# A transformer block on one core: score rows of a pair's two heads on separate halves of the partitions

## The reference

```python
ada = silu(c) @ W_ada + b_ada                      # 6 vectors of 288 for each sequence
shift_msa, scale_msa, gate_msa, shift_mlp, scale_mlp, gate_mlp = split(ada, 6)
h = layernorm(x) * (1 + scale_msa) + shift_msa
q, k, v = split(h @ W_qkv + b_qkv)                 # 16 heads, D = 18
attn = softmax((q * D**-0.5) @ k.T)                # 256 x 256 for each head
x = x + gate_msa * ((attn @ v) @ W_proj + b_proj)
h = layernorm(x) * (1 + scale_mlp) + shift_mlp
x = x + gate_mlp * (gelu(h @ W_fc1 + b_fc1) @ W_fc2 + b_fc2)   # FF = 1152
```

## Time and profile before

| | |
|---|---|
| median of 3 runs | 1230.65 us (1229.91 to 1230.84) |
| time of the profiled execution | 1228.32 us |
| its span | 1226.5 us |
| TensorE busy | 96% of the span; weight loads 87% |
| VectorE, ScalarE, GpSimd busy | 74%, 71%, 44% |

### The profile page before, as it was taken

How to read it: one execution, slowest core, us unless ns; L and a number is a source line. 1 busy time by engine, 2 the same in 40 slices (tenths; PEclk the granted TensorE clock), 3 DMA queues, 4 the chain that set the end, 5 groups by cost and what they waited for, 6 DMA issues and landing times.

```text
span 1226.5 us, 27564 instructions
## 1 busy us (share of the span) xinstructions
PE 1181.1 (96%) x9863; PEld 1064.3 (87%) x9863; DVE 901.8 (74%) x1928; ACT 866.1 (71%) x1485; POOL 540.3 (44%) x557
## 2 busy tenths in 40 slices
PE   6888999999999999999999999999999999999977
PEld 5666999999998999999999999999999999997777
DVE  5687777877777787778777777777777787775553
ACT  5387777777777777777777777777777777778721
POOL 3012544444454444445454444444444445443364
PEclk9799999999999999999999999999999999999999
DMA  8554555554555554445555444555554555444220
GB/s 265 171 169 138 167 167 164 164 154 144 163 160 159 168 166 145 157 157 162 167 166 164 147 159 150 166 165 167 161 153 148 158 166 159 162 149 140 87 68 20
DMA packets 134330, 188.91 MB, mean 154 GB/s; under 512 B 24544, under 2 KB 102422, under 8 KB 133947
## 3 DMA queue, kind: packets, MB, share of 16 engines
q1 hardware_dynamic: 134033, 186.71, 48.3%
q10 hardware_dynamic: 162, 0.44, 0.1%
HBM read 121.92 MB, written 64.63 MB: 152 GB/s over the span
## 4 chain that ended last, share of the span: by engine, by line
PE 84%; SPq 5%; DMA 4%; DVE 3%; ACT 2%; issue 1%; POOL 0%; ACTq 0%; POOLq 0%; DVEq 0%
PE a_bank L867 10%; PE x_bank L785 10%; PE score_bank L808 9%; PE turn_bank L834 9%; PE st_bank L822 9%; PE b_bank L867 8%; PE b_bank L881 6%; PE b_bank L882 5%; PE b_bank L883 5%; PE a_bank L848 4%; PE x_bank L793 4%; SPq L623 2%; DMA qk_rows<-qst 1%; DMA ql<-zeros 1%; PE x_bank L759 1%
## 5 line engine op out<-in xcount | busy, mean ns | idle before, releaser
L1138 DVE TENSOR_REDUCE mx<-score_bank 128x2 f32<-128x512 f32 x512 | 342.0, 687 | 95.8 <-PE score_bank L808 93.7
L953 ACT ACTIVATE e<-st_bank 128x1024 f32<-128x1024 f32 x256 | 262.4, 1025 | 125.8 <-PE st_bank L822 123.5
L1287 POOL TENSOR_TENSOR gl<-gl_raw,gh 128x512 fp32r<-128x512 f32 (+1 forms) x160 | 194.3, 1221 | 226.4 <-DVE gh L1203 226.4
L946 ACT CAST ql<-mxt 4x256 fp32r<-4x256 f32 x512 | 206.2, 403 | 7.4 <-DVE mxt L1147 0.6
L808 PEld LDWEIGHTS score_bank<-kl,ql 122*128 122x128 f32 x1024 | 146.9, 190 | 42.0 <-issue 24.4
L808 PE MATMUL score_bank<-kl,ql 122*128 122x256 f32 x1024 | 174.6, 293 | 5.6 <-DMA ql<-zeros 3.3
L881 PE MATMUL b_bank<-w,gh 128*128 128x288 f32 x576 | 174.5, 303 | 2.2 <-DVE tmp L1209 1.9
L822 PE MATMUL st_bank<-ql,kl 122*128 122x512 f32 x512 | 165.7, 405 | 7.7 <-ACT e L953 6.9
L882 PE MATMUL b_bank<-w,gh 128*128 128x288 f32 x576 | 170.5, 296 | 0.0
L883 PE MATMUL b_bank<-w,gl 128*128 128x288 f32 x576 | 170.3, 296 | 0.0
L834 PE MATMUL turn_bank<-e,ve 128*32 128x256 f32 x2048 | 123.8, 382 | 0.3 <-ACT e L953 0.3
(11 more groups left out here) (152 smaller groups left out, 2473.1 us busy)
## 6 DMA issues: line engine op xcount, KB each, us to landing
qk_rows<-qst SPq DMA_DIRECT2D x128, 256.0 KB, 5.3
ql<-qk_rows SPq DMA_DIRECT2D x384, 72.0 KB
kl<-qk_rows SPq DMA_DIRECT2D x378, 72.0 KB
o_rows<-on SPq DMA_DIRECT2D x128, 128.0 KB
gate<-gates SPq DMA_DIRECT2D x32, 432.0 KB, 4.4
xin<-in_x SPq DMA_DIRECT2D x32, 288.0 KB, 5.9
x<-in_x SPq DMA_DIRECT2D x32, 288.0 KB, 3.0
out<-x SPq DMA_DIRECT2D x32, 288.0 KB, 4.5
```

The costliest lines, as they stand in the source:

```text
L946: last = nc.scalar.copy(rows[:, :, :, t, a, :], src)
L953: nc.scalar.activation(e[:, j % 4, :, :, :].rearrange("p u i l -> p (u i l)"), st_bank[:, :, :, :].rearrange("p u i l -> p (u i l)"), ACT. ...
L1138: nc.vector.tensor_reduce(mx[:, j // HP, i, :, col:col + 1], score_bank[i][:, :].rearrange("p (t l) -> p t l", t=NT), AX.X, ALU.max).then_ ...
L1287: nc.gpsimd.tensor_tensor(gl[:, cols], g[:, cols], gh[:, cols].bitcast(F32), ALU.subtract).then_inc(g_lo, 1)
```

## The change

What it does:

- A tile of 64 partitions for each head of a pair (TILE = 64): rows 0 to 3 of a tile are the max rows, rows 4 to 57 the q or k rows, KM = 58. Head 0 has partitions 0 to 57, head 1 partitions 64 to 121. ql no longer holds the heads apart and no longer has zeros for the other head, so its slot is half as large.
- s: four matmuls as before, of 58 rows each, in the order head 0, head 1, head 0, head 1. st: four matmuls of 256 columns instead of two of 512, heads in turn as well. The two heads of a pair write different banks of PSUM.
- Four slots instead of three. The thirteenth read (zeros) is gone, READS = 12, with its memory buffer. In its place GpSimd clears 68 partitions x 1024 of the slot, in a new step **clr** (twice in a period, after ln2_stats), which waits until the st steps of the half that used the slot are done. qkr waits for clr.
- kl's max rows are set once, at the start, by four ScalarE copies over 68 partitions in place of four small DMAs.
- mb: eight copies of 4 partitions as before, sorted by head instead of by row tile.
- The order of the steps on all engines is unchanged but for clr and for what qkr no longer has.

```diff
-MXR = 64
-HB = MXR + PAIRS // 2
-KM = HB + KS
+TILE = 64
+KM = PAIRS // 2 + KS
-SLOTS = 3
+SLOTS = 4
-READS = 13
+READS = 12
...
 POOL_ORDER = [
...
-    ("proj", -1, 0), ("proj", -1, 1), ("sum2", -2, 0), ("ln2_stats", -1, 0), ("bias", -1, 0), ("lt", -1, 0),
-    ("sum2", -2, 1), ("xt", 3, 0), ("fc1", -1, 0),
+    ("proj", -1, 0), ("proj", -1, 1), ("sum2", -2, 0), ("ln2_stats", -1, 0), ("clr", 2, 0), ("clr", 2, 1),
+    ("bias", -1, 0), ("lt", -1, 0), ("sum2", -2, 1), ("xt", 3, 0), ("fc1", -1, 0),
...
-        ql = sb("ql", [P, SLOTS, 2, HP, L], F32R)
+        ql = sb("ql", [P, SLOTS, HP, L], F32R)
-        e = sb("e", [P, 4, NT, 2, L])
+        e = sb("e", [P, 4, 2, NT, L])
...
-                    if use == 0:
-                        sp.wait_ge(consts, ROWS_SET)
-                        wait(sp, rows_cleared, slot)
-                    else:
-                        before = b * HALVES + half - SLOTS
-                        sp.wait_ge(st_full, PAIRS * (before // HALVES) + HP * (before % HALVES + 1))
-                if m == 12:
...
-                        sp.dma_start(ql[MXR:MXR + HP, slot, :, :, :].rearrange("p i j l -> p (i j l)").bitcast(F32),
-                                     zero_dram).then_inc(qk_rows[slot], 16)
-                    return
+                    if b == 0 and half == 0:
+                        sp.wait_ge(kl_chosen, SLOTS)
+                    sp.wait_ge(ql_cleared, HALVES * b + half + 1)
...
                 for i in range(2):
                     wait(pe, s_max[i], PAIRS * b + j)
-                    for t in range(NT):
+                for t in range(NT):
+                    for i in range(2):
+                        rows = slice(TILE * i, TILE * i + KM)
                         last = nc.tensor.matmul(score_bank[i][:, t * L:(t + 1) * L],
-                                                ql[0:KM, slot, i, j % HP, t * P:(t + 1) * P], kl[0:KM, slot, j % HP, :],
+                                                ql[rows, slot, j % HP, t * P:(t + 1) * P], kl[rows, slot, j % HP, :],
                                                 start=True, stop=True)
-                    last.then_inc(s_full[i], 1)
+                        if t == NT - 1:
+                            last.then_inc(s_full[i], 1)
...
                 for u in range(NT):
-                    last = nc.tensor.matmul(st_bank[:, u, :, :], kl[0:KM, slot, j % HP, u * P:(u + 1) * P],
-                                            ql[0:KM, slot, :, j % HP, :], start=True, stop=True)
+                    for i in range(2):
+                        rows = slice(TILE * i, TILE * i + KM)
+                        last = nc.tensor.matmul(st_bank[:, i, u, :], kl[rows, slot, j % HP, u * P:(u + 1) * P],
+                                                ql[rows, slot, j % HP, :], start=True, stop=True)
                 last.then_inc(st_full, 1)
...
+            def clear(b, half):
+                slot, use = half_use(b, half)
+                if use:
+                    before = b * HALVES + half - SLOTS
+                    pool.wait_ge(st_full, PAIRS * (before // HALVES) + HP * (before % HALVES + 1))
+                    nc.gpsimd.memset(ql[0:TILE + HP, slot, :, :].bitcast(F32), 0.0).then_inc(ql_cleared, 1)
```

More of the change, by code:

```diff
@@ L158 @@
     ("ln1_stats", 0, 0), ("xt", 0, 0), ("ln1_stats", 1, 0), ("xt", 1, 0), ("ln1_stats", 2, 0), ("xt", 2, 0),
[4 rows of a table removed]
+    ("ln1_stats", 3, 0), ("clr", 2, 0), ("clr", 2, 1), ("xt", 3, 0), ("ln1_stats", 4, 0), ("ol", 0, 0),
+    ("proj", 0, 0), ("proj", 0, 1), ("ln2_stats", 0, 0), ("clr", 3, 0), ("clr", 3, 1), ("xt", 4, 0), ("lt", 0, 0),
+    ("fc1", 0, 0), ("bias", 0, 0), ("fc1", 0, 1), ("ln1_stats", 5, 0), ("fc1", 0, 2), ("ol", 1, 0), ("fc1", 0, 3),
+    ("fc1", 0, 4), ("proj", 1, 0), ("proj", 1, 1), ("sum2", 0, 0), ("ln2_stats", 1, 0), ("clr", 4, 0), ("clr", 4, 1),
+    ("bias", 1, 0), ("lt", 1, 0), ("sum2", 0, 1), ("xt", 5, 0), ("fc1", 1, 0),
 ]
@@ L383, in dit_block @@
         minus_rows = sem("minus_rows")
-        kl_rows = sem("kl_rows")
         w_split = sem("w_split")
@@ L529, in qk_row @@
             c0 = half * HALF_ROWS + (w * 2 + i) * D * HP
-            row = (0, HB)[i] + D * r
-            to = ql[row:row + D, slot, i, :, :] if w == 0 else kl[row:row + D, slot, :, :]
+            row = TILE * i + HP + D * r
+            to = (ql if w == 0 else kl)[row:row + D, slot, :, :]
             return (to.rearrange("p j l -> p (j l)").bitcast(F32),
@@ L698, in _ @@
                 load_weights(i)
-            sp.wait_ge(consts, ROWS_SET)
-            for jj in range(HP):
-                row = slice(MXR + jj, MXR + jj + 1)
-                sp.dma_start(kl[row, :, jj, :].bitcast(F32),
-                             tmp2[row, 0, 0:L].unsqueeze(1).broadcast_to([1, SLOTS, L])).then_inc(kl_rows, 16)
-            sp.dma_start(zero_dram, ql[MXR:MXR + HP, 0, :, :, :].rearrange("p i j l -> p (i j l)").bitcast(F32)
-                         ).then_inc(zeros_stored, 16)
             run(SYNC_HEAD, SYNC_ORDER, SYNC_TAIL, {"ln1_stats": ln1_stats, "res": res, "qkw": qkw, "qkr": qkr, "ow": ow,
@@ L903, in _ @@
             act.wait_ge(iota_step, 2)
-            for slot in range(1, SLOTS):
-                nc.scalar.activation(ql[:, slot, :, :, :].rearrange("p i j l -> p (i j l)"),
-                                     ident[:, 0:1].broadcast_to([P, 2 * HP * L]), ACT.Copy, scale=0.0
-                                     ).then_inc(rows_cleared, 1)
+            act.wait_ge(choice, 1)
+            for slot in range(SLOTS):
+                nc.scalar.activation(kl[0:TILE + HP, slot, :, :],
+                                     chosen[0:TILE + HP, :].unsqueeze(2).broadcast_to([TILE + HP, HP, L]), ACT.Copy,
+                                     scale=-1.0).then_inc(kl_chosen, 1)
             for i in range(N_FIRST):
@@ L941, in mb @@
                 act.wait_ge(mx_turned, HALVES * b + half + 1)
-                rows = ql[MXR:MXR + HP, slot, :, :, :].rearrange("p i j (t a x) -> p i j t a x", t=NT, x=VB)
-                for t in range(NT):
+                for i in range(2):
+                    rows = ql[TILE * i:TILE * i + HP, slot, :, :].rearrange("p j (t a x) -> p j t a x", t=NT, x=VB)
                     for a in range(P // VB):
-                        src = mxt[VB * a:VB * a + HP, half, :, t, :].unsqueeze(2).broadcast_to([HP, 2, HP, VB])
-                        last = nc.scalar.copy(rows[:, :, :, t, a, :], src)
+                        src = mxt[VB * a:VB * a + HP, half, i, :, :].unsqueeze(1).broadcast_to([HP, HP, NT, VB])
+                        last = nc.scalar.copy(rows[:, :, :, a, :], src)
                 last.then_inc(mx_rows, 1)
@@ L1302, in _ @@
             run(POOL_HEAD, POOL_ORDER, POOL_TAIL, {"ln1_stats": ln1, "ln2_stats": ln2, "xt": xt, "lt": lt, "ol": ol_sub, "proj": proj,
-                             "bias": bias,
+                             "bias": bias, "clr": clear,
                              "fc1": fc1, "sum2": sum2})
```

106 lines of the change are left out of this document (50 added, 56 removed), and 19 rows, old and new, of tables (POOL_HEAD, SYNC_TAIL).

## The result

The changed kernel takes **1255.01 us** (median of four runs, 1249.88 to 1261.06), the kernel before, measured with it, 1230.74: ratio **1.018 [1.015, 1.021]**. Five more runs gave 1251.22 and 1.013 [1.011, 1.016]. The first four runs fall in two clusters, 1250 and 1251 us at a mean granted clock of 0.980, and 1259 and 1261 at 0.967; the profiled execution lies in the shorter one. The prediction was 1231, with a range up to 1253. The first median lies outside that range, the second just inside it.

A forecast was written before the change was run, and what follows sets the result against it. TensorE's sequence of matmuls was taken to bound the kernel. Terms of -117.3, +122.2, -2.9 and, for reads, -1.5 us sum to +0.5, so 1231 us was predicted from a median of 1230.65, range 1218 to 1253.

The forecast's parts named there:

- The two steps themselves: TensorE's s and st steps: both heads' matmuls run at once on separate halves of the array, saving 117.3 us.
- B: Rival for s and st: halves run abreast but slower than one stream, giving 1244 up to 1251 us; chance 0.17.
- C: Rival for s and st: the halves don't overlap while tile changes remain, giving 1348 to 1350 us; chance 0.10.
- The change of tile: TensorE switching between full- and half-height matmuls: 627 added changes, 0.20 us each (0.15 before transpositions), costing 122.2 us.
- Rival D: Tile changes on TensorE cost less between halves than read, giving 1178 us, or 1205 if only leaving is cheap; chance 0.15.
- Late weights: TensorE's st steps whose weights arrive too late to hide: that wait falls inside the tile-change drain, saving 2.9 us.
- Costed at nothing: GpSimd's clears, mb, exponential, maxima and start: covered by idle time or existing waits, so 0 us.
- Both maxima before s: s needs both heads' maxima before its first matmul: put at nothing, as TensorE waited 0.6 us for them in all.
- The head: Start of the kernel: four ScalarE copies over 1024 columns replace two over 2048, GpSimd clears less; put at nothing.

The follow-up runs named there:

- st0_dma: dma_clears with st of pair 0 moved right behind s of pair 4, ahead of a third of fc2; 1234.37 us, ratio 1.000.
- dma_clears: Changed kernel with GpSimd's clears after the start replaced by two DMA writes of zeros behind each half's last read; 1242.81 us, ratio 1.007.
- hold_only: dma_clears, still without GpSimd memsets, but SyncE's reads wait until GpSimd reaches the places where the changed kernel cleared; 1250.55 us, ratio 1.015.
- port_only: dma_clears plus same-size GpSimd memsets into an unread buffer at the changed kernel's clear places, SyncE not waiting; 1244.47 us, ratio 1.010.
- heads_apart: Changed kernel with head 0's two matmuls issued before head 1's, in s each behind its own maxima; 1252.34 us, ratio 1.014.
- regroup2_dma: dma_clears with st of pair 0 right behind s of pair 4, and s of pairs 1 to 3 one place later; 1214.78 us, ratio 0.985.
- fill_dma: dma_clears plus matmuls without a use in seven gaps of TensorE's head between 60 and 100 us; 1246.43 us, ratio 1.008.

## Why the prediction was wrong

- **The two steps themselves (-117.3): right.** The two heads start 3 ns apart in the median (7 was taken), and a step behind another takes 234 ns, or 117 a slot. Rivals B and C are out.
- **The change of tile (+122.2): right, to the hundredth.** Full to half costs 0.194 us, half to full 0.197 to 0.200, half to a transposition 0.14 to 0.15, by the ends of the matmuls on both sides. A lone step takes 0.432 us where 0.235 + 0.007 + 0.20 = 0.44 was expected; st0_dma gave 0.194 for each change. Rival D is out.
- **Late weights (-2.9): right.** The st step in front of proj, which took 0.58 us in the median before, takes the 0.43 of every other first step in dma_clears.
- **The sum of the middle.** With no idle time left, dma_clears moves away from the kernel before by 5.1 us in 26 sequences, 0.20 each. The prediction's own prices, counted for one sequence of the steady part, make 0.13: 18 changes at 0.20 and 2 at 0.15, less 3.66 for its 16 steps and 0.11 for the late weights. By the ends of the matmuls, everything but one step comes out 0.2 us cheaper than that, at about -0.1 a sequence (st took 0.473 before and not 0.465, a change costs 0.194 to 0.20, and one st step of the kernel before took 1.86 us); the one step adds 0.30 (told under "Both maxima before s").
- **Costed at nothing: the step that failed.** "Queued behind a clear's wait for st_full are bias, lt and sum2 ... so the wait is over on arrival" looked at GpSimd's list alone, and was right there but for one wait of 9.5 us in the head. It left out that the change also adds a wait for the clears to SyncE, and what stands behind that in SyncE's queue: the sums, the reciprocals' rows, o's rows. The cover named for the clears was GpSimd's idle time behind rs, but a clear placed there comes later than a read in SyncE's queue wants it. hold_only prices this at 0.8%, some 10 us in the medians (dma_clears 1.007, hold_only 1.015) and 3.9 us in the profiled spans. Without the clears on GpSimd the time, 1242.81, lies inside the predicted range. The tail shows the same chain as the head (VectorE, changed kernel):

```profile
1122.80 1.52 DVE L1052 TENSOR_SCALAR xn<-x,mv,rs 128x288 f32<-128x288 f32 x1
...
1131.06 0.35 DVE L1143 RECIPROCAL rc<-sums 64x32 f32<-64x32 f32 x1 [3.98 <-DMA sums<-on]
```

  The reciprocal waits 3.98 us for the sums, and fc1 behind it 2.3 us. The first row is the stalled apply, and s behind it waits 1.31 us. That stall is the second thing left out: a cover on GpSimd's own list isn't free while VectorE wants what GpSimd holds. At the changed kernel's places port_only, with two thirds of the stalled time, prices it at 0.3%, within the error; the early places took 18 us more than the late ones.
- **Both maxima before s (nothing, 0.6 us of waits before): another term that failed.** The list of waits hides its size, since it is the weights of s that wait and TensorE is hardly idle. It shows in one group of each sequence, an st and an s step among fc2's matmuls. The chain of the changed kernel and VectorE's row, then VectorE's row of the kernel before (start, us, what):

```profile
607.87 0.43 PE st_bank L808 x4
608.30 0.03 issue
608.33 0.50 PE score_bank L791 x4
...
607.51 0.68 DVE L1126 TENSOR_REDUCE mx<-score_bank 128x2 f32<-128x512 f32 x1
```

```profile
633.14 0.68 DVE L1138 TENSOR_REDUCE mx<-score_bank 128x2 f32<-128x512 f32 x1
```

  The maxima of head 1 end 0.32 us behind the matmul ahead of st (608.19, 607.87); in the kernel before it was 0.24 us (633.82, 633.58), and s needed them only for its third matmul, whose weights were loaded 0.41 us behind. Now the first weights of s wait for both maxima. In the other groups of st and s they load 0.15 us behind the matmul ahead of the group, here 0.43 us, and s takes 0.53 us instead of 0.23, where it took 0.47 as ever before. The group takes 967 ns instead of 667 in dma_clears and in the changed kernel alike, in each of 26 sequences, 7.8 us in the middle. In heads_apart, where head 0's weights load at 0.16 us and only head 1's matmuls wait, it takes 869, and in regroup2_dma, whose maxima come earlier, 668. Without this wait the halves would have gained about 2.7 us in the middle. Of the 8.2 us of idle time for maxima on the changed kernel's page, 3.4 are the held queue.
- **The head (nothing).** In dma_clears pv 7 is already 5.4 us late. Its clock from 46 to 121 is 0.86 (1.00 before). In the head TensorE waits for maxima and exps, so shorter steps buy nothing there, only idle time; the clock is at its lower level for stretches behind such idle time, and what runs in them takes longer (a pv step of the changed kernel there takes 3.19 us, elsewhere 1.9). That the clock holds all of the 5 us was argued and not shown: fill_dma couldn't tell.

Together, in the profiled spans (21.6 us): halves in the head 5.4, in the middle 5.1 (7.8 for the maxima, less 2.7), in the tail 2; clears 9, of which the tail holds 5. The prices that the prediction read from TensorE's trace came out; the loss came from waits between the engines that were put at nothing.

## What to carry to other kernels

When work moves to another engine, look for every engine that must now wait for it, and price what stands behind that wait in its queue; the idle time of the engine that does the work says nothing about when the others need it. Where half-height matmuls alternate with full ones, count the changes of tile at 0.2 us and put such steps side by side: the same halves went from 0.7% slower to 1.5% faster by the order of the lists alone. When a step comes to need all its inputs before its first matmul, compare the time when its first weights are loaded with the end of its last input; a wait that falls on the weights hardly shows as idle time. Before moving a ScalarE function between others, see which table it uses.

## What the runs showed of the hardware that was not expected

- Matmuls on separate halves of the rows overlap without being issued in turn: with head 0's two ahead of head 1's two, the matmuls of a lone step still pair up, 7 ns apart (9 at most), and the step takes 436 ns instead of 432.
- A vector instruction that needs what GpSimd holds isn't let in between GpSimd's instructions if these follow each other without a pause: 4.13 us for an apply that takes 0.79 in the median of the changed kernel (the same shape 0.42 where GpSimd is idle), over two subtractions, one more and the end of a clear. The maxima that read PSUM were not held (694 against 684 ns).
